# Layer 0 attention of a conv-attention hybrid: product with a diagonal matrix in place of scale and transpose, and scores issued in pairs

## The reference, cut to what matters

```
k_win = k[:, :, idx_h][:, :, :, :, idx_w]          # 7 x 7 window around each token
v_win = v[:, :, idx_h][:, :, :, :, idx_w]
attn = jnp.einsum('bhijc,bhikjlc->bhijkl', q, k_win)
attn = attn + bias.transpose(0, 1, 3, 2, 4)[None]
attn = jax.nn.softmax(attn.reshape(B, nh, H, W, K * K), axis=-1)
attn = attn.reshape(B, nh, H, W, K, K)
out = jnp.einsum('bhijkl,bhikjld->bhijd', attn, v_win)
```

## Time and profile before

| what | value |
|---|---|
| median of 3 runs | 10392.46 us (10381.14 to 10393.34) |
| span of the profiled execution, first to last instruction | 10375.5 us |
| PE busy in the span | 8825.9 us (85%) |
| DVE, ACT, POOL busy | 5783.3 us (56%), 4145.5 us (40%), 3261.0 us (31%) |
| attention of layer 0, first to last score | 451.1 to 2475.9 us, 928 units |

### The profile page before, as it was taken

One profiled execution on the slowest core, in us unless ns is written; L12 is line 12 of the kernel. 1 busy time (PEld: TensorE's weight loads), 2 busy tenths in 40 slices (PEclk: granted clock), 3 DMA queues, 4 the chain that ended last, 5 costly groups with the idle time before them and its releaser, 6 DMA issues. The chain is left out here.

```text
span 10375.5 us, 158377 instructions
## 1 busy us (share of the span) xinstructions
PE 8825.9 (85%) x47072; PEld 4663.3 (45%) x47072; DVE 5783.3 (56%) x13683; ACT 4145.5 (40%) x9073; POOL 3261.0 (31%) x1854
## 2 busy tenths in 40 slices
PE   4499989997667999998999989999999885448888
PEld 3355545554444444444444444444444334325555
DVE  4355555555557976675766757766676004324444
ACT  1255555553000055555555555555555660001111
POOL 2000000000000055555555555555555670142211
PEclk8655555555876599999999999999999996569999
DMA  4511121101533001202112021111211004211110
GB/s 137 88 20 20 20 35 20 20 8 49 178 123 103 10 20 28 56 21 56 27 24 56 19 56 30 31 45 30 47 28 41 14 5 127 78 40 42 44 34 21
DMA packets 368839, 480.22 MB, mean 46 GB/s; under 512 B 154040, under 2 KB 322362, under 8 KB 354855
## 3 DMA queue, kind: packets, MB, share of 16 engines
q1 hardware_dynamic: 344551, 426.24, 17.0%
q0 software_dynamic: 23424, 43.45, 1.6%
HBM read 298.80 MB, written 180.34 MB: 46 GB/s over the span
## 5 line engine op out<-in xcount | busy, mean ns | idle before, releaser
L1057 POOL TENSOR_TENSOR a_added<-a_P 128x896 f32<-128x896 f32 x1344 | 2805.3, 2107 | 3517.1 <-ACT a_P L1029 3516.8
L935 DVE TENSOR_REDUCE a_tops<-a_ps 128x1 f32<-128x448 f32 x5600 | 3166.2, 632 | 1322.8 <-PE a_ps L843 1319.5
L1029 ACT ACTIVATE a_P<-a_ps 128x448 f32<-128x448 f32 (+1 forms) x5600 | 2610.3, 548 | 2600.3 <-PE a_ps L901 2599.3
L901 PE MATMUL a_ps<-a_qp,a_kp 98*128 98x448 f32 (+1 forms) x5600 | 1946.8, 399 | 171.4 <-DMA a_qp<-scratch_neg 97.9
L843 PE MATMUL a_ps<-a_hk,a_hq 96*128 96x448 f32 (+1 forms) x4900 | 1922.6, 406 | 118.9 <-DMA a_hk<-scratch_k 96.8
L843 PEld LDWEIGHTS a_ps<-a_hk,a_hq 96*128 96x128 f32 (+1 forms) x4900 | 917.7, 188 | 1205.3 <-DVE a_tops L935 1047.2
L901 PEld LDWEIGHTS a_ps<-a_qp,a_kp 98*128 98x128 f32 (+1 forms) x5600 | 1008.0, 189 | 951.7 <-ACT a_P L1029 637.8
L860 PE MATMUL a_ps<-a_P,a_vt 128*32 128x448 f32 (+1 forms) x11200 | 1362.2, 558 | 0.0
L459 DVE CUSTOM_DVE_ANT_0 n_sm<-n_ps,n_bias 112x448 f32<-112x448 f32 x928 | 578.1, 624 | 850.8 <-PE n_ps L390 850.8
L485 ACT ACTIVATE n_P<-n_sm,n_mx 112x448 f32<-112x448 f32 x928 | 620.2, 668 | 845.4 <-DVE n_mx L459 845.4
L400 PE MATMUL n_ps<-n_idn,n_P 112*112 112x112 f32 x3712 | 923.5, 404 | 21.5 <-DVE n_P L466 21.5
(11 more groups left out here) (174 smaller groups left out, 6476.7 us busy)
## 6 DMA issues: line engine op xcount, KB each, us to landing
a_qp<-scratch_q SPq DMA_DIRECT2D x168, 224.0 KB, 3.8
a_hq<-scratch_q SPq DMA_DIRECT2D x84, 392.0 KB, 7.3
a_hk<-scratch_k SPq DMA_DIRECT2D x84, 392.0 KB, 8.6
a_kp<-scratch_k SPq DMA_DIRECT2D x96, 320.0 KB, 4.9
scratch_t<-o_ts SPq DMA_DIRECT2D x8, 3136.0 KB, 13.2
e_w<-in_w SPq DMA_DIRECT2D x16, 1024.0 KB
p_xs<-in_x SPq DMA_DIRECT2D x4, 3136.0 KB, 15.3
scratch_v<-p_vs SPq DMA_DIRECT2D x4, 3136.0 KB, 12.5
```

The costliest lines, as they stand in the source:

```text
L901: pe.matmul(PS[0:rows_of(t), i_s % 3, 0:GW], kp[0:98, hh, 128 * t:128 * t + rows_of(t)], qp[0:98, hh, GW * j:GW * j + GW], start=True, sto ...
L935: dve.tensor_reduce(tops[0:rows_of(t), KT * hh + t, k:k + 1], PS[0:rows_of(t), MAX + i % MAXES, 0:GW], AX_X, ALU.max).then_inc(topped, 1)
L1029: act.activation(P[0:rows_of(t), (2 * n + pair) % (2 * RING), hh % 2, :], PS[0:rows_of(t), (4 * n + hh) % 3, 0:GW], ACT.Exp).then_inc(expe ...
L1057: pool.tensor_tensor(added2[:, a % 6, :, :], P[:, (2 * n + pair) % (2 * RING), :, :], P[:, (2 * n + 2 + pair) % (2 * RING), :, :], ALU.add ...
```

## The change

It does four things in `layer0_attend`.

- P is no longer scaled in place. DVE scales the identity instead, 112 columns, into one of ND = 4 tiles `diag`, and PE multiplies the block of P with it: `P.T @ diag(1/sum)` is the transposed and normalised block. The instruction is a float32 product, where it was a transpose.
- The scores of units n and n + 1 (n even) are issued together, in two different row strips and two banks. Scores now have 4 banks (0 to 3), and in an even step n PE waits on `maxed` for unit n - 3.
- Transposed blocks have 2 banks (4 and 5) in place of 3: the products of unit m wait on `copied` for unit m - 2.
- The identity is loaded first, and DVE waits for it before its memsets; before, it was loaded after the first pass's data.

```diff
-        BS, BT, BO = 0, 3, 6
+        NSM, NP, NPT, ND = 4, 6, 12, 4
+        BS, BT, BO = 0, 4, 6
...
+        diag = sb("diag", [TT, ND, TT])
...
             sp.sem_inc(stored, 16)
+            sp.dma_start(idn[:, :], A["eye"][0:TT, 0:TT]).then_inc(consts, 16)
             sp.wait_ge(zeroed, 2)
             load(0, 0, None)
-            sp.dma_start(idn[:, :], A["eye"][0:TT, 0:TT]).then_inc(consts, 16)
             load_bias(0)
...
                 for n in range(4 * QT + MIX):
-                    if n < U:
+                    if n < U and n % 2 == 0:
                         r, hh = divmod(n, 4)
-                        if n >= 3:
+                        if n >= 4:
                             pe.wait_ge(maxed, it * U + n - 2)
-                        rows = slice(32 * hh, 32 * hh + 16)
-                        pe.matmul(PS[0:TT, BS + n % 3, 0:KW].rearrange("p (c s t) -> p c s t", c=4, s=SUB),
-                                  qp[rows, TT * r:TT * r + TT],
-                                  kp[rows, :, TR * kv[r]:TR * kv[r] + 56].rearrange("p s (c t) -> p c s t", c=4),
-                                  start=True, stop=True).then_inc(scored, 1)
+                        for h in (hh, hh + 1):
+                            rows = slice(32 * h, 32 * h + 16)
+                            pe.matmul(PS[0:TT, BS + h, 0:KW].rearrange("p (c s t) -> p c s t", c=4, s=SUB),
+                                      qp[rows, TT * r:TT * r + TT],
+                                      kp[rows, :, TR * kv[r]:TR * kv[r] + 56].rearrange("p s (c t) -> p c s t", c=4),
+                                      start=True, stop=True).then_inc(scored, 1)
                     if TURN <= n < U + TURN:
                         m = n - TURN
                         pe.wait_ge(normed, it * U + m + 1)
-                        if m >= 3:
-                            pe.wait_ge(copied, it * U + m - 2)
+                        if m >= 2:
+                            pe.wait_ge(copied, it * U + m - 1)
                         for c in range(4):
-                            last = pe.transpose(PS[0:TT, BT + m % 3, TT * c:TT * c + TT],
-                                                P[:, m % NP, TT * c:TT * c + TT], idn[:, :])
+                            last = pe.matmul(PS[0:TT, BT + m % 2, TT * c:TT * c + TT],
+                                             P[:, m % NP, TT * c:TT * c + TT], diag[:, m % ND, :],
+                                             start=True, stop=True)
                         last.then_inc(turned, 1)
...
+            dve.wait_ge(consts, 16)
             dve.memset(qn[:, :, :], 0.0).then_inc(zeroed, 1)
...
                             dve.wait_ge(inverted, it * U + m + 1)
-                            dve.tensor_scalar(P[:, m % NP, :], P[:, m % NP, :], rc[:, m % 8:m % 8 + 1], None,
+                            if m >= ND:
+                                dve.wait_ge(turned, it * U + m - ND + 1)
+                            dve.tensor_scalar(diag[:, m % ND, :], idn[:, :], rc[:, m % 8:m % 8 + 1], None,
                                               ALU.mult).then_inc(normed, 1)
```

More of the change, by code:

```diff
@@ L294, in layer0_attend @@
         INVERT, NORM, TURN, COPY, MIX, READ = 2, 3, 4, 5, 9, 14
-        NSM, NP, NPT = 4, 6, 12
-        BS, BT, BO = 0, 3, 6
+        NSM, NP, NPT, ND = 4, 6, 12, 4
+        BS, BT, BO = 0, 4, 6
         idn = sb("idn", [TT, TT])
@@ L457, in _ @@
                             dve.sem_inc(steps, 1)
-                            dve.tensor_tensor_reduce(out=sm[:, n % NSM, :], in0=PS[0:TT, BS + n % 3, 0:KW],
+                            dve.tensor_tensor_reduce(out=sm[:, n % NSM, :], in0=PS[0:TT, BS + n % 4, 0:KW],
                                                      in1=bias[:, hh, case_of(r), :], scale=1.0, scalar=3.0e38,
@@ L491, in _ @@
                             act.wait_ge(mixed, it * QT + (m - NPT) // 4 + 1)
-                        act.activation(PTs[:, m % NPT, :], PS[0:TT, BT + m % 3, 0:KW], ACT.Copy).then_inc(copied, 1)
+                        act.activation(PTs[:, m % NPT, :], PS[0:TT, BT + m % 2, 0:KW], ACT.Copy).then_inc(copied, 1)
                 act.wait_ge(mixed, (it + 1) * QT)
```

## The result

The changed kernel takes 10676.05 us (median of 3, 10642.2 to 10677.04) against 10392.46: 1.027 of before, 95% interval 1.025 to 1.029. It is slower by 284 us, where 10,228 had been forecast with a range to 10,430.

A forecast was written before the change was run, and what follows sets the result against it. PE at half clock was taken to bound layer 0's attention; with the clock rising to full, -175, -10 and +20 us sum to -165, so 10392.5 - 165 = 10228 us, range 10,140 to 10,430.

The forecast's parts named there:

- What bounds the kernel: Layer 0's attention: PE at half clock bounds the stage, busy 222.85 of 225 us, with 2.10 us a unit.
- the sum: Over all passes: -175 us from 856 steps, -10 at pass ends, +20 for half clock at pass starts; -165 in all.
- The blocks' products: A unit's blocks on PE: 1.67 us in place of 0.92 at half clock, 0.91 us at full clock.
- Rival (d): PE's weight loads do not quicken at full clock: 2.27 us a unit, +140 us, 10,530; chance 0.04.
- The scores in pairs: PE's scores: a pair costs what one costs, 0.65 us in place of 1.30 at half clock, 0.41 at full.
- The loop through the copy: At full clock PE's blocks wait 0.94 us for ACT's copy, 2.57 us from the pair's start; a pair takes 3.79.
- Rival (c): ACT reaches the copy sooner, so it does not hold PE: 1.43 us a unit, 9,830; chance 0.02.
- So I take it that it stays: In layer 0's attention, full clock, once reached, holds despite gaps, as in layer 1 over 3700 to 3900; forecast's chance 0.70.
- rival (b): PE's clock rises and falls again under the 0.94 us stall: 10,476 with half the time at each level; chance 0.13.
- Some 10 us into each pass: PE's clock rises some 10 us into each pass; half clock until then costs +20 us in all.
- Rival (a): PE's clock stays at half all through: 2.53 us a unit against 2.10, +410 us, 10,800; chance 0.11.
- The rest: DVE's shorter scale, off the loop, is worth nothing; loading the identity first costs 0, within 3 us.

The follow-up runs named there:

- v1: The changed kernel with ACT's copy put ahead of its exponential in each step; 9907 us, 0.957 of before.
- v7: v1 with PE's work for two units grouped (scores, all blocks, all value products) and the stages further apart; 9788 us, 0.942 of before.
- v11: v10 with the second transposes only in the first 32 units of a pass; 9606 us, 0.929 of before.
- v8: v7 with transposes and the scale in place instead of products with the diagonal; 9942 us, 0.956 of before.
- v10: v8 with every block transposed twice into the same place; 9768 us, 0.940 of before.

## Why the prediction was wrong

- **What bounds the kernel:** right. PE at half clock was the bound. Only the reading of the slices was loose: slices 2 and 6 of PE show 4 and 8 tenths, not nine, as the stage begins within slice 2; the windows and the step, on which the sum rests, are read rightly.
- **The blocks' products:** right in kind. Blocks take 1.76 us at half clock (1502.62 - 1500.86) where 1.67 was forecast, and 0.97 at full (1526.31 - 1525.34) where it was 0.91. The records follow each other nearly as read: 16 of them last 3.33 us in v1 where 8 last 1.83, at half clock, which is 0.187 each, and 1.82 against 1.04 at full clock (v7 and the changed kernel), which is 0.098. The start of each run, which I had taken over from the transposes, is about 0.1 us longer at half clock: a weight load of these products takes 0.30 us on average, one of the transposes took 0.20. Rival (d), loads that keep their pace, is excluded: at full clock the eight loads take 0.86 us.
- **The scores in pairs:** right; both in 0.71 us, 0.65 to the next part, 0.42 at full clock.
- **The loop through the copy:** right, found from the step of before, where it was hidden. 2.65 to 2.68 us against 2.57, a pair 3.95 against 3.79. Rival (c) is excluded by the 0.90 us of idle.
- **"So I take it that it stays":** this step failed. The clock did rise, as forecast, but it fell again and again, which was rival (b), given 0.13. I had read from 3700 to 3900 of layer 1 that full clock bears gaps between groups. But there PE is idle for 3.3 of 200 us in all, with one wait of 1.2 us, and my own sum had just put 0.94 us into every 3.79. v1 shows the reverse of that step: take the wait away and PEclk goes from 0.66 to 0.89.
- **"Some 10 us into each pass":** too early for the first pass. Its first score is at 459.7, the clock is 0.50 up to 496, up for a few us behind that, 0.50 again over 500 to 527, and 1.00 over 528 to 554. The sum had put +20 us at this start for all passes.
- **Rival (b)'s price:** too low, as it took half of the pairs at each level with 5.05 and 3.79 us. With a third of the time at full clock, and 5.23 and 3.95 for a pair, the +250 of above comes out, 10,640 for the median before; what is then missing lies outside of the pairs.
- **Rival (a):** it gave 10,800 for a clock that stays low all through; the stage was at half clock for two thirds of its time, and the 10,676 measured lie between the forecast of 10,228 and this.
- **The rest:** DVE's scale fell from 0.45 to 0.27 us and gained nothing, as forecast. The identity cost 1.7 us of idle and at most 3.3 in all, where 3 were allowed.

Even at full clock throughout the change would have gained 464 pairs x 0.25 = 116 us, 1.1%, and not the 165 of the sum, as the blocks and the loop took longer than forecast (3.95 us a pair against 3.79). v1, with the wait gone and the clock mostly up, gained 431 (10338 - 9907).

## What to carry to other kernels

When an engine's clock depends on its own load, price a wait twice: once for its length, and once for what it does to the clock; at half clock this one did not show at all. When buffers are moved from one use to another, walk the loop that the smaller ring closes, and ask which instruction of the reader stands in front of the one that frees the buffer: swapping two independent instructions was worth 7% here, more than the change that they served. And in this kernel less work held TensorE's clock, once it was up, than it took to lift it (v11 against v8).

## What the runs showed that I had not expected

None of this stood in the prediction; the later runs were built to test it.

- Work that computes nothing new can pay: v10 does twice the transposes of v8 and is 1.7% faster (0.940 of before against 0.956), v11 does so for 32 of 116 units and is 2.9% faster (0.929).
- The level depends on what came before: v8 and the later part of v11's passes issue the same instructions in the same order, one at 3.22 us a pair and 0.50, the other at a mean of 2.4 us and 1.00.
- What in the changed kernel lifts the clock, at times, where v8 with its three parts a pair in place of five stays at half, is left open; no run here tried it.
